# Attention with new buffers, order and start; mamba's skip term on VectorE and GpSimd instead of TensorE

## What is computed

```python
# attention: 16 heads of 16; W.. with the adapter of the sequence, chosen from lora_start_indices
Q, K, V = (_multilora(x, ids, W, A, B) for W, A, B in ((Wq, Aq, Bq), (Wk, Ak, Bk), (Wv, Av, Bv)))
Q, K = _rope(split(Q)), _rope(split(K))
scores = where(causal, einsum('bhqd,bhkd->bhqk', Q, K) / sqrt(16), -inf)
out = einsum('bhqk,bhkd->bhqd', softmax(scores), split(V))
return _multilora(out, ids, Wo, Ao, Bo)

# mamba: 8 heads of 64, state of 128
z, xBC, dt = parts of einsum('bld,de->ble', x, w_in)
dt = softplus(dt + dt_bias)
xh, Bm, Cm = parts of silu(conv(xBC) + conv_b)
y = _ssd(xh * dt[..., None], dt * -exp(A_log), Bm, Cm)
y = y + xh * D[None, None, :, None]              # the skip term
y = y.reshape(B, L, 512) * silu(z)
y = y * rsqrt(mean(y * y) + EPS) * norm_w
return einsum('ble,ed->bld', y, w_out)
```

## Time and profile before

| | us |
|---|---|
| median of 3 runs | 2264.7 |
| lowest and highest of them | 2252.42, 2266.2 |
| the profiled execution | 2262.66 |
| its span in the profile | 2260.9 |
| mean granted clock of TensorE, as a share of 2.4 GHz | 0.876 |
| TensorE busy (matmuls) | 1903.7 (84%) |
| TensorE busy (weight loads) | 1261.6 (56%) |
| VectorE busy | 1232.5 (55%) |
| ScalarE busy | 792.0 (35%) |
| GpSimd busy | 738.7 (33%) |

### The profile page before, as it was taken

The page is one execution under the profiler, slowest core; times in us unless marked ns, Lnnn a source line. Parts: engine busy times, 40 slices in busy tenths (PEclk is TensorE's granted clock), DMA queues, the critical chain, the costliest instruction groups (busy, mean ns, idle before and its releaser), DMA issues. The chain is left out here.

```text
span 2260.9 us, 29368 instructions
## 1 busy us (share of the span) xinstructions
PE 1903.7 (84%) x9520; PEld 1261.6 (56%) x9520; DVE 1232.5 (55%) x2967; ACT 792.0 (35%) x1321; POOL 738.7 (33%) x934
## 2 busy tenths in 40 slices
PE   5478888889888885399999928989989857999997
PEld 3143434334343333288888824747565645888886
DVE  4356666656665753843434445656566676434342
ACT  2035444554544453311111105454455551111111
POOL 3525362643535231122222222423333222222221
PEclk8559788986986988699999968999899987999999
DMA  6422332422333212600000031010101062000000
GB/s 186 141 82 95 95 106 75 138 76 92 97 97 119 77 31 86 238 22 25 24 29 26 16 111 75 1 75 1 75 1 76 1 244 72 25 27 25 29 23 9
DMA packets 85552, 160.67 MB, mean 71 GB/s; under 512 B 18456, under 2 KB 45852, under 8 KB 84256
## 3 DMA queue, kind: packets, MB, share of 16 engines
q1 hardware_dynamic: 67424, 108.18, 14.1%
q0 software_dynamic: 17984, 50.62, 7.0%
HBM read 102.26 MB, written 45.22 MB: 65 GB/s over the span
## 5 line engine op out<-in xcount | busy, mean ns | idle before, releaser
L652 ACT ACTIVATE a_probs<-a_ps_e 128x1024 f32<-128x1024 f32 (+3 forms) x384 | 303.3, 812 | 262.3 <-PE a_ps_e L808 257.9
L796 PE MATMUL a_ps_m<-a_k_st,a_q_st 64*128 64x512 f32 (+3 forms) x768 | 249.3, 446 | 110.2 <-DVE a_peak L412 50.6
L412 DVE CUSTOM_DVE_ANT_0 a_ps_m<-a_ps_m,a_causal 128x512 f32<-128x512 f32 (+3 forms) x512 | 241.9, 512 | 118.5 <-PE a_ps_m L796 117.1
L1387 PE MATMUL g_ps_y<-g_w_d,x_res 128*128 x1120 | 253.3, 379 | 2.7 <-DVE x_res L1157 2.7
L416 DVE TENSOR_REDUCE a_peak<-a_ps_m 128x1 f32<-128x512 f32 x256 | 170.4, 687 | 137.7 <-PE a_ps_m L796 136.4
L796 PEld LDWEIGHTS a_ps_m<-a_k_st,a_q_st 64*128 64x128 f32 x768 | 138.2, 228 | 184.8 <-DVE a_peak L412 87.0
L1387 PEld LDWEIGHTS g_ps_y<-g_w_d,x_res 128*128 128x128 f32 x1120 | 212.3, 190 | 34.5 <-issue 3.2
L535 POOL TENSOR_SCALAR_AFFINE_SELECT a_probs<-a_probs 128x256 f32<-128x256 f32 x256 | 103.1, 408 | 376.0 <-ACT a_probs L652 372.1
L808 PE MATMUL a_ps_e<-a_q_st,a_k_st 64*128 64x512 f32 (+3 forms) x768 | 205.8, 482 | 7.6 <-DMA a_q_st<-a_low_and_less 5.6
L808 PEld LDWEIGHTS a_ps_e<-a_q_st,a_k_st 64*128 64x128 f32 x768 | 96.9, 217 | 200.5 <-issue 125.6
L824 PE MATMUL a_ps_a<-a_probs,a_vals 128*32 128x512 f32 (+3 forms) x1536 | 202.8, 607 | 2.2 <-POOL a_probs L535 2.2
(11 more groups left out here) (269 smaller groups left out, 3719.3 us busy)
## 6 DMA issues: line engine op xcount, KB each, us to landing
a_q_st<-a_scr_q POOLq DMA_DIRECT2D x32, 512.0 KB, 4.0
a_k_st<-a_scr_k POOLq DMA_DIRECT2D x32, 512.0 KB, 4.9
m_spread_acs<-m_acs_rows SPq DMA_DIRECT2D x8, 2048.0 KB, 9.3
a_scr_q<-a_high SPq DMA_DIRECT2D x36, 256.0 KB
a_scr_k<-a_high SPq DMA_DIRECT2D x36, 256.0 KB
a_swapped<-a_raw SPq DMA_DIRECT2D x64, 128.0 KB, 2.1
g_w_gu<-L_ffn_Wg SPq DMA_DIRECT2D x8, 1024.0 KB, 12.0
g_w_gu<-L_ffn_Wu SPq DMA_DIRECT2D x8, 1024.0 KB, 14.0
```

Source lines behind the costliest of these rows:

```text
L412: nc.vector.tensor_tensor_reduce(ps_m[:, bank, 0:w], ps_m[:, bank, 0:w], causal[:, 512 - w:], 1.0, MASKED, ALU.add, ALU.max, peak[:, p % 2 ...
L652: nc.scalar.activation(probs[:, N % RING, :, q0:], ps_e[:, N % 2, :, q0:], ACT.Exp, scale=DH ** -0.5).then_inc(exp_done, 1)
L796: nc.tensor.matmul(bank[:, 0:w], q_st[rows(r), p % BUFS, i * P:(i + 1) * P], k_st[rows(r), p % BUFS, 512 * c:512 * c + w], start=True, sto ...
L1387: last = nc.tensor.matmul(ps_y[:, 0:D], hid_t[:, f * P:(f + 1) * P], w_d[:, bass.ds(e, 1), f].rearrange("p a d -> p (a d)"), start=(f == 0 ...
```

## The change

In attention:

- `ps_m` gets 4 banks. `ps_e` becomes a ring of 3 single banks (`HEAD_BANKS`), one head each: step N's two matmuls use two of them, and are issued once the exponential of the first head of step N-1 has ended. ScalarE runs an exponential per head, 768 in place of 384, and semaphores count heads.
- Chunks are issued in pairs (both halves r), with both banks free before the first; `CUTS` is rounded to even numbers.
- Denominators: 8 rows of 512 are gathered as 128 x 32 (`gather_sums`), inverted there, stored (`store_inverse`) and loaded spread (`spread_inverse`). Steps of the unit at which this happens: gather 13 or 4, inversion 17 or 7 (was 18 or 8), store 18 or 8, spread 20 or 10, `scale` 23 or 13 (was 20 or 10). `project_out` of the first two pieces waits for the first half of the queries only.
- Start: W first, then x in two halves, then B, on SyncE; start indices and A, and behind the copies of W rope, on ScalarE's queue; x of the other sequences behind the stores of block 0. Block 0 is rotated on VectorE (`turn_first`), GpSimd keeps the remainders; the first root goes ahead of the choice of adapters, and the others behind the first four loads of q and k.

In mamba: `skips` and `skip_m` go. VectorE multiplies the input in ps_t by D into `xskip`, right behind xdt; TensorE's next `tokens` waits for it. GpSimd adds xskip to y in `gate`, waits for its own addition, and then multiplies by the gate. D comes in one load, not two.

The diff, cut to its core:

```diff
-    BANKS = 3
+    BANKS = 4
+    HEAD_BANKS = 3
...
-        return min(TOTAL, 2 * NC * whole + sum(x <= at - whole for x in chunk_at))
+        return min(TOTAL, 2 * NC * whole + sum(x <= at - whole for x in chunk_at) // 2 * 2)
...
-        ps_e = ctx.enter_context(nc.psum_tensor("a_ps_e", [P, 2, 2, 512], F32))
+        ps_e = ctx.enter_context(nc.psum_tensor("a_ps_e", [P, HEAD_BANKS, 512], F32))
...
+            def gather_sums(U, c):
...
+                sp.dma_start(sums[:, c], sums_d[B % 2, c].rearrange("a u (k q) -> (a u k) q", q=32)
+                             ).then_inc(sums_in[c], 16)
+            def store_inverse(B, c):
+                sp.wait_ge(inverted, 2 * B + c + 1)
+                sp.dma_start(inverse_d[B % 2, c].rearrange("u (k q) -> (u k) q", q=32), sums[:, c]
+                             ).then_inc(inverse_out[c], 16)
+            def spread_inverse(B, c):
+                sp.wait_ge(inverse_out[c], 16 * (B + 1))
...
             def invert(B, c):
-                dve.wait_ge(den_in[c], 16 * (B + 1))
-                nc.vector.reciprocal(den[:, c], den[:, c]).then_inc(inverted, 1)
+                dve.wait_ge(sums_in[c], 16 * (B + 1))
+                nc.vector.reciprocal(sums[:, c], sums[:, c]).then_inc(inverted, 1)
+            def turn_first(i):
+                dve.wait_ge(swap_in[i], 32)
+                nc.vector.tensor_tensor(raw[:, i], raw[:, i], rope[:, 0, half], ALU.mult).then_inc(dve_step, 1)
...
...
-            for i in range(4):
-                for part in range(3):
-                    rotate(0, i, part)
-                if i >= 1:
-                    remainder(0, i - 1)
-            remainder(0, 3)
+            for i in range(4):
+                remainder(0, i)
+            for p in range(4):
+                load(p)
             for b in range(1, BATCH):
                 inverse_std(b)
-            for p in range(4):
-                load(p)
...
             def exponential(U, n):
-                act.wait_ge(shifted_ps, N + 1)
-                nc.scalar.activation(probs[:, N % RING, :, q0:], ps_e[:, N % 2, :, q0:], ACT.Exp, scale=DH ** -0.5
-                                     ).then_inc(exp_done, 1)
+                for r in range(2):
+                    act.wait_ge(shifted_ps, 2 * N + r + 1)
+                    nc.scalar.activation(probs[:, N % RING, r, q0:], ps_e[:, (2 * N + r) % HEAD_BANKS, q0:], ACT.Exp,
+                                         scale=DH ** -0.5).then_inc(exp_done, 1)
...
             def shifted(U, n):
-                if N >= 2:
-                    pe.wait_ge(exp_done, N - 1)
+                if N >= 1:
+                    pe.wait_ge(exp_done, max(2 * N + 2 - HEAD_BANKS, 1))
...
             def project_out(b, i):
-                pe.wait_ge(normed, 4 * b + 4)
+                pe.wait_ge(normed, 4 * b + 3 + i // 2)
...
             def inputs(b, t):
                 nc.vector.tensor_tensor(xdt[:, t % 2], by_head(ps_t[:, 0]), heads(dt[:, t]), ALU.mult
                                         ).then_inc(xdt_ready, 1)
+                if N >= 2:
+                    dve.wait_ge(skipped, N - 1)
+                nc.vector.tensor_tensor(xskip[:, t % 2], by_head(ps_t[:, 0]), heads(skip[:]), ALU.mult
+                                        ).then_inc(xskip_ready, 1)
...
             def gate(b, t):
                 pool.wait_ge(y_sum, N + 1)
+                pool.wait_ge(xskip_ready, N + 1)
+                nc.gpsimd.tensor_tensor(y[:, t % 2], y[:, t % 2], xskip[:, t % 2], ALU.add).then_inc(skipped, 1)
+                pool.wait_ge(skipped, N + 1)
                 nc.gpsimd.tensor_tensor(y[:, t % 2], y[:, t % 2], by_head(z_act[:, t]), ALU.mult).then_inc(y_ready, 1)
...
-            def skips(b, t):
-                for k in range(ZT):
-                    nc.tensor.matmul(ps_y[:, 0, k * P:(k + 1) * P], xbc[:, k, s], skip_m[:, k], start=(k == 0), stop=False,
-                                     skip_group_check=True)
             def diagonal(b, t):
-                                           start=False, stop=True, skip_group_check=True)
+                                           start=True, stop=True)
```

More of the change, by code:

```diff
@@ L258, in attention @@
         out_in = [sem(f"out_in{c}") for c in range(2)]
+        sums_in = [sem(f"sums_in{c}") for c in range(2)]
+        inverse_out = [sem(f"inverse_out{c}") for c in range(2)]
         den_in = [sem(f"den_in{c}") for c in range(2)]
@@ L269, in _ @@
             x = A["x"]
[L270 removed]
             for m, name in enumerate("qkvo"):
                 sp.dma_start(w_nat[:, m], A["W" + name].rearrange("(t p) d -> p t d", p=P)).then_inc(w_in, 16)
+            for half in range(2):
+                sp.dma_start(X[:, half * HALF:(half + 1) * HALF], x[:, half * HALF:(half + 1) * HALF]
+                             ).then_inc(x_in[0], 16)
+            for m, name in enumerate("qkvo"):
                 for t in range(2):
                     sp.dma_start(b_nat[:, m, t], A["B" + name][:, t * P:(t + 1) * P, :].rearrange("e p r -> p e r")
[L275 to L279 removed]
+                                 ).then_inc(b_in, 16)
             sp.wait_ge(scr_ready, 2)
@@ L285, in _ @@
                                      high[:, n]).then_inc(scr_filled, 16)
-            for b in range(1, BATCH):
-                sp.dma_start(X[:, b * T:(b + 1) * T], x[:, b * T:(b + 1) * T]).then_inc(x_in[b], 16)
             def swap(blk, i):
@@ L330, in _ @@
                 keep(0, i)
+            for b in range(1, BATCH):
+                sp.dma_start(X[:, b * T:(b + 1) * T], x[:, b * T:(b + 1) * T]).then_inc(x_in[b], 16)
             for i in range(4):
@@ L790, in scores @@
             def scores(k):
-                p, (i, c, r) = k // NC, CHUNKS[k % NC]
-                bank = bank_of(("chunk", k))
+                p, (i, c, _) = k // NC, CHUNKS[k % NC]
+                banks = [bank_of(("chunk", k + r)) for r in range(2)]
                 if k % NC == 0:
@@ L795, in scores @@
                 w = width(k)
-                nc.tensor.matmul(bank[:, 0:w], q_st[rows(r), p % BUFS, i * P:(i + 1) * P],
-                                 k_st[rows(r), p % BUFS, 512 * c:512 * c + w], start=True, stop=True).then_inc(score_ps, 1)
+                for r in range(2):
+                    nc.tensor.matmul(banks[r][:, 0:w], q_st[rows(r), p % BUFS, i * P:(i + 1) * P],
+                                     k_st[rows(r), p % BUFS, 512 * c:512 * c + w], start=True, stop=True
+                                     ).then_inc(score_ps, 1)
             def shifted(U, n):
@@ L830, in _ @@
                 piece(e)
-            for k in range(CUTS[0]):
+            for k in range(0, CUTS[0], 2):
                 scores(k)
-                if k in AMID:
-                    piece(AMID[k])
+                if k + 1 in AMID:
+                    piece(AMID[k + 1])
             for U in range(UNITS):
@@ L838, in _ @@
                     shifted(U, n)
-                    for k in range(issued_after(N - 1), issued_after(N)):
+                    for k in range(issued_after(N - 1), issued_after(N), 2):
                         scores(k)
@@ L1512, in _ @@
                 sp.dma_start(conv_w[:], M["conv_w"].rearrange("(t p) k -> p t k", p=P)).then_inc(loaded, 16)
-                for k in range(2):
-                    sp.dma_start(skip[k * HDIM:(k + 1) * HDIM, :],
-                                 M["D"].rearrange("(a t two) -> two a t", a=1, two=2)[k].to_broadcast([HDIM, ZT])
-                                 ).then_inc(loaded, 16)
             sp.dma_start(dt_bias[:], spread(M["dt_bias"])).then_inc(loaded, 16)
             sp.dma_start(a_neg[:, 0], spread(M["A_log"])).then_inc(loaded, 16)
+            sp.dma_start(skip[:], spread(M["D"])).then_inc(loaded, 16)
             for b in range(BATCH):
```

147 lines of the change are left out of this document (84 added, 63 removed).

## The result

The changed kernel takes 2202.4 us (median of 4, 2191.66 to 2203.91) against 2258.6 for the kernel before (median of 4, 2250.92 to 2266.2): ratio 0.974, 95% interval 0.970 to 0.979. Forecast were 2199 and a range of 2150 to 2262. The total is close; the sum behind it is not, as the stages show. The medians differ by 56 us and the two profiled spans by 71.

A forecast was written before the change was run, and what follows sets the result against it. It took a load chain to bound the start, TensorE at a low clock, interrupted by VectorE, steady attention, and TensorE with a near-equal GpSimd chain mamba; -12 - 35 + 0 - 25 + 1 + 5 = -66, predicting 2199 us, range 2150 to 2262.

The forecast's parts named there:

- Reciprocals and clock, -35 and -25: Steady attention: shorter reciprocals save 35 us (-42 to 0); half the low-clock and transfer-wait cost returns, 25 us (-50 to 0).
- Rival (c): Steady attention: denominators' three transfers come late, VectorE waits as long as before, reciprocals and clock give 0; 2259 us, chance 0.10.
- Banks, 0 between -25 and +47: Steady attention: new banks, pairing and three-bank ring net 0 us; bounds -25 (waits saved) and +47 (ring waits, nothing regained).
- (a): Steady attention: ring of three banks eats the gain, +47 for 0 and clock -10 for -25; 2259 us, chance 0.13.
- (b): Steady attention: ring waits in every step hold TensorE at the low clock, clock +67, ring +47; 2338 us, chance 0.09.
- Start, -12: Start of attention: reordered loads, block 0 rotated on VectorE and roots moved give 18 us, less 6; net -12 (-20 to -4).
- I take back 6: Start of attention: 6 us lost to late x loads sharing engines with q and k, and statistics before the first maximum.
- End, +1: End of attention: ScalarE bound +4, reciprocal saving 3.0, two more transfers, output projection -3; net +1 us (-5 to +6).
- My own 1.16 us: Steady attention: latency from an odd step's shifted pair to the next, against 0.90 us of work between.
- -3 for the output projection: End of attention: half of the output projection no longer waits for the last denominators, -3 us.
- Mamba, +5: Mamba: chain through GpSimd grows to 7.94 us per tile despite less TensorE work; net +5 us (-28 to +15).
- rival (d): Mamba: TensorE is the bound and gets its relief, -28 for +5; 2166 us, chance 0.08.

The follow-up runs named there:

- recip_alone: The kernel before with only the gathered 128x32 reciprocals added (gather, inversion, store, spread): 2206.4 us, ratio 0.977 to the kernel before.
- old_banks: The changed kernel with the former banks: 3 for chunks issued singly, 2 pairs for shifted scores, one exponential for both heads: 2226.3 us, ratio 0.986.
- four_three: The changed kernel with 4 single banks for the shifted scores and 3 for the chunks, pairs kept: 2264.6 us, ratio 1.005.
- x_early: The changed kernel with the other sequences' x loads issued right behind the eight stores of constants: 2192.4 us, ratio 0.974.
- weigh_early_pe: The changed attention with mamba as before (skip term on TensorE), but GpSimd weighing ahead of gate and root: 2205.3 us, ratio 0.977.
- old_mamba: The changed attention with mamba as before, the skip term on TensorE: 2190.3 us, ratio 0.972.
- spread_later: The changed kernel with the first query half's inverted denominators spread in step 3 and multiplied in step 7 of the next unit: 2198.1 us, ratio 0.973.

## Why the prediction was right, and where it was not

**Reciprocals and clock, -35 and -25: right as a sum of 60.** Taken back, they cost 55 us; made alone, they give 2.3% of 2253, some 51. The waits for maxima fell from 64.0 us (49.4 of the earlier trace rows and 14.6 of the chunks without a mask) to 25.9 in recip_alone, 38 us for the term of 35; that leaves 13 to 17 for the clock's 25. The low clock behind a long stall is seen in the earlier trace rows. But at 1.2 GHz were 270 us of the steady part before, 677.5 x 0.17 / 0.5 = 230 in recip_alone, and 619.8 x 0.10 / 0.5 = 124 in the change: most of that fall came only with the new banks. Rival (c), the three transfers late, didn't happen for VectorE, whose wait it spoke of (3.4 us in the steady part for the gathered sums, 10.4 for the spread ones before); it happened for the rows of maxima, a wait that I did not name.

**Banks, 0 between -25 and +47: the step that failed.** They give some 24 us in the whole, and 33 to 42 in the steady part (709.4 to 676.8, 661.4 to 619.8), more than my bound of 25. The sizes that I gave were right. Three periods of two wide steps take 9.18 us in the changed kernel, 3.06 each for 3.12; the latency is 1.24 us for 1.16; the ring's waits are 39.5 us in 110 places, 47 set down.

```profile
701.22 0.51 PE L854 MATMUL a_ps_e<-a_q_st,a_k_st 64*128 64x512 f32 x2
...
704.04 0.50 PE L854 MATMUL a_ps_e<-a_q_st,a_k_st 64*128 64x512 f32 x2
...
705.28 0.50 PE L854 MATMUL a_ps_e<-a_q_st,a_k_st 64*128 64x512 f32 x2 [0.51 <-ACT a_probs L690]
...
710.40 0.50 PE L854 MATMUL a_ps_e<-a_q_st,a_k_st 64*128 64x512 f32 x2
```

At the full clock the new banks are indeed worth nothing. Units 1 and 14 ran at 1.00 in old_banks too, and took 38.2 and 30.1 us, for 37.7 and 30.5 in the change:

```profile
190.90:229.10 38.20, 35.19 (x213) 14.60 (x213) 26.57 (x86) 23.77 (x35) 25.59 (x37) 1.00 0.39 122
769.60:799.70 30.10, 26.35 (x191) 11.78 (x193) 21.93 (x74) 20.01 (x28) 11.58 (x24) 1.00 0.19 56
```

TensorE is busy for less of unit 1 in the change (33.0 us for 35.2) and idle for more. The gain lies in the units that run in part at the low clock: unit 4 takes 49.8 us for 54.7 (clock 0.77 and 0.81), unit 13 31.6 for 41.6 (1.00 and 0.63). At 1.2 GHz were 661.4 x 0.15 / 0.5 = 198 us in old_banks, for 124. This isn't one execution's luck: the nine kernels with new banks and short reciprocals have a clock of 0.89 to 0.91 in the steady part, the two with the old banks 0.83 and 0.85. My sum had banks and clock as two terms, and let only the stalls of the reciprocals act on the clock; that was the mistake. Why the clock falls less often isn't shown. TensorE's waits aren't fewer (88.6 us in 175 places; 71.7 in 120 in old_banks).

What the fourth bank does for the chunks is seen against four_three, which has the pairs too (and a ring of four): units 1 and 5, at 1.00, take 40.3 and 40.4 us there, for 37.7 and 38.1. Pairs without the fourth bank lose; the fourth bank without pairs wasn't run.

Rivals (a) and (b) are refuted: the ring's waits are there in 110 places, and the unit that answers to the earlier trace rows runs at 1.00, for 0.95. The rule of the Trainium skill that I weighed there (TensorE: Matmul & The Clock Gate, A second HAM failure mode: psum-queue depth-cycling) stays open here. It has frequent short idle times make the clock swing. From the kernel before to the change TensorE's waits rose from 126 to 175 and the clock rose too, which speaks against it. But in recip_alone the granted clock fell from 1.00 to 0.50 for 30.7 us behind 15 us in which no wait of TensorE was over 0.6 us:

```profile
713.00:728.00 15.00, 13.32 (x91) 7.26 (x93) 10.73 (x31) 7.57 (x12) 5.94 (x14) 1.00 0.25 74
728.00:758.70 30.70, 29.93 (x123) 11.91 (x115) 17.27 (x59) 12.86 (x16) 4.74 (x11) 0.50 0.16 49
```

**Start, -12: wrong, and hidden by another error.** The q/k projection came 5.6 us earlier, not 10 (37.48 to 31.86), the first loads 10.1, not 18. (The difference that I put at 11 is 20.3 - 8.3 = 12; it changes little.) "I take back 6" for x was the mis-sized term: TensorE alone stood for 13.9. With three banks for the chunks the new start makes unit 0 later than before (138.3 in old_banks, 141.8 in four_three, against 130.5). The fourth bank shortens the stage of the first chunks from 60.9 and 64.1 to 55.0, and so unit 0 came out at 129.8, even. (The two kernels with three banks are one execution each; seven with the fourth bank and the same start reach unit 0 at 129.8 to 133.2.) Neither was in my sum. With the loads of x early, the same start reaches unit 0 at 115.7.

**End, +1: the wrong bound.** I took ScalarE's rate, 24 x 0.17. It was the ring's latency, bare because the last unit has no chunks to cover it: the steps took 32.7 us for 22.0. My own 1.16 us, applied to 24 steps of 0.92, would have given half of it (5.8). The rest goes with a lower clock, 0.75 in this stage for 0.80 before; where the same ring met a clock of 0.60, in x_early, the steps took 39. How much the clock alone costs isn't shown. The -3 for the output projection didn't come: from the last shifted scores to the next stage it was 29.7 and is 29.6.

**Mamba, +5: the tile was right, the first tile missing.** The chain of 7.92 is the forecast's 7.94, and rival (d), TensorE's relief of 28, was closed by this chain; with the chain opened, 15 us of it appeared against the kernel before, and 23 against weigh_early_pe. The missing term is the first interval of each batch: the longer chain leaves TensorE idle for 3 us, the clock falls, and the interval grows by 2.1 to 2.8 and not by 0.46; four of them are 10 us. The last interval of a batch, put at -0.88, grew in two of three batches; it varies by itself (10.2 to 13.6 in old_mamba). I used the clock for attention and forgot it here: TensorE is busy for 424.1 us in the stage, 5.4 less than before and not 28, and 488.6 x 0.10 / 0.5 = 98 us of it are at 1.2 GHz, by the same sum 57 before.

## What to carry to other kernels

A long instruction on one engine costs the matmul engine its own length and then the low clock behind it: look for such waits first. A bank is worth what its users wait for: the fourth one gained with the paired chunks, and lost when it went to the exponentials instead. And don't read the worth of such an edit at the full clock alone: here it was nothing there, and all of it appeared where part of the time runs at the low clock. Where a chain through a slow engine is as long as the tile, moving work to that engine pays only if its order is changed with it: put what the next matmul needs ahead of what only the output needs. Price a latency where its cover ends (the first tile, the last unit, the first load), not only where it is hidden.

## What the runs showed of the hardware

- A wait of TensorE of 2.96 us, after a tile at the high level, was followed by 5.2 us at a granted clock of 0.54, near 1.2 GHz, with full work. Units 1 and 13 of the change, with short waits only, stayed at 1.00. But short waits aren't always harmless: in recip_alone 30.7 us at 0.50 followed 15 us without a wait over 0.6.
- In the start, two VectorE operations of 0.69 us took 1.64 and 1.43 while GpSimd took a remainder. The Trainium skill (SBUF — State Buffer, SBUF: two separate sides) says that a VectorE operation with two inputs in SBUF and a GpSimd operation that reads SBUF share a pair of ports, which one of them holds for its whole instruction; these rows agree, each VectorE operation ending 0.55 us behind GpSimd's.

```profile
40.74 1.35 POOL L546 TENSOR_TENSOR a_low<-a_raw,a_high 128x512 f32<-128x512 f32 x1 [16.25 <-ACT a_high L674]
...
41.00 1.64 DVE L468 TENSOR_TENSOR a_raw<-a_raw,a_swapped 128x512 f32<-128x512 f32 x1
```

- Two rows of 1024 values took 7 us from issue to landing when a broadcast of 128x512 was issued 0.03 us behind them, and at most 5.1 in spread_later, where it wasn't (218.91 to 224.01, when TensorE's wait of 1.5 us for them ended).
